# Window attention on one core: 196 padded keys replaced by a few keys that carry logarithms of exponential sums

## The reference

```python
h = layer_norm(x, ln1_g, ln1_b)
hp = jnp.pad(h, ((0, 0), (0, pad_h), (0, pad_w), (0, 0)))     # after the norm: padded keys have k = bias
qkv = win.reshape(Bw, N, C) @ qkv_w + qkv_b                    # win: 32 windows of N = 196 tokens
attn = jnp.einsum('bnd,bmd->bnm', q * scale, k)
bias_h = jnp.einsum('bhwc,hkc->bhwk', rq, Rh)                  # q times a table of row distances
bias_w = jnp.einsum('bhwc,wkc->bhwk', rq, Rw)                  # the same for column distances
attn = attn + bias_h[..., :, None] + bias_w[..., None, :]
o = jax.nn.softmax(attn, axis=-1) @ v
x2 = shortcut + o @ proj_w + proj_b
out = x2 + gelu(layer_norm(x2, ln2_g, ln2_b) @ mlp_w1 + mlp_b1) @ mlp_w2 + mlp_b2
```

## Time and profile before

| | us |
|---|---|
| median of three runs | 259.3 |
| profiled execution, own time | 261.9 |
| its span | 260.1 |
| PE busy | 243.9 (94%) |
| DVE busy | 170.0 (65%) |
| ACT busy | 128.9 (50%) |
| POOL busy | 114.7 (44%) |

### The profile page before, as it was taken

How to read it: one execution, slowest core, us unless ns; L and a number is a source line. 1 busy time by engine, 2 the same in 40 slices (tenths; PEclk the granted TensorE clock), 3 DMA queues, 4 the chain that set the end, 5 groups by cost and what they waited for, 6 DMA issues and landing times.

```text
span 260.1 us, 5439 instructions
## 1 busy us (share of the span) xinstructions
PE 243.9 (94%) x1996; PEld 190.5 (73%) x1996; DVE 170.0 (65%) x477; ACT 128.9 (50%) x216; POOL 114.7 (44%) x180
## 2 busy tenths in 40 slices
PE   7499999999799999999998989979999999999995
PEld 3245568897677777778666866658878889798994
DVE  3996839336988989988789997528977391400011
ACT  2157698436366565765657556630646451604100
POOL 4449775914116568866576653561310570000000
PEclk9889999999889999999999999977999999999999
DMA  6645214787127886777766633392000001000011
GB/s 173 188 112 138 51 36 114 177 203 174 40 66 175 188 185 168 185 178 181 196 168 152 165 82 90 97 272 70 0 0 3 0 0 61 3 30 32 14 49 62
DMA packets 22232, 27.80 MB, mean 107 GB/s; under 512 B 7287, under 2 KB 18409, under 8 KB 22205
## 3 DMA queue, kind: packets, MB, share of 16 engines
q1 hardware_dynamic: 18253, 21.37, 31.4%
q0 software_dynamic: 3424, 5.89, 9.8%
q10 hardware_dynamic: 528, 0.20, 0.3%
HBM read 5.84 MB, written 1.57 MB: 29 GB/s over the span
## 4 chain that ended last, share of the span: by engine, by line
PE 68%; DMA 11%; DVE 8%; ACT 6%; POOL 3%; issue 2%; SPq 1%; DVEq 0%; ACTq 0%; POOLq 0%
PE ps L1485 12%; PE ps L1469 8%; PE ps L1150 7%; PE ps L1259 7%; PE ps L1301 6%; PE ps L1325 5%; DMA qop<-shift 3%; DVE bias L923 3%; PE ps L1224 3%; PE ps L1382 2%; PE ps L1369 2%; DMA wq<-in_qkv_w 2%; PE ps L1330 2%; PE ps L1265 2%; DMA qop<-bias 2%
## 5 line engine op out<-in xcount | busy, mean ns | idle before, releaser
L942 DVE TENSOR_REDUCE nmax<-ps 98x2 f32<-98x392 f32 x96 | 52.6, 562 | 16.9 <-PE ps L1259 14.9
L737 ACT ACTIVATE pm<-ps 98x784 f32<-98x784 f32 x48 | 38.9, 826 | 23.6 <-PE ps L1301 23.5
L1259 PE MATMUL ps<-kop,qop 126*98 126x196 f32 x192 | 37.1, 278 | 2.1 <-DVE nmax L942 1.4
L1259 PEld LDWEIGHTS ps<-kop,qop 126*98 126x98 f32 x192 | 25.8, 168 | 9.2 <-issue 3.8
L1485 PE MATMUL ps<-w2t,gl 128*128 128x192 f32 x192 | 31.7, 326 | 0.0
L1485 PEld LDWEIGHTS ps<-w2t,gl 128*128 128x128 f32 x192 | 31.4, 190 | 0.3
L808 ACT ACTIVATE gl<-ps,vec 128x512 f32<-128x512 f32 x24 | 16.1, 686 | 30.1 <-PE ps L1469 30.1
L1301 PE MATMUL ps<-qop,kop 128*98 128x196 f32 x192 | 27.4, 266 | 0.9 <-DMA qop<-shift 0.9
L1106 DVE TENSOR_TENSOR xn<-ps,xres 128x384 f32<-128x384 f32 x8 | 4.5, 557 | 31.1 <-PE ps L1485 31.1
L1150 PE MATMUL ps<-ht,bias 128*128 128x512 f32 x48 | 22.8, 625 | 1.4 <-POOL bias L491 1.4
L1301 PEld LDWEIGHTS ps<-qop,kop 128*98 128x98 f32 x192 | 21.9, 170 | 2.7 <-DMA qop<-shift 1.3
(11 more groups left out here) (162 smaller groups left out, 500.9 us busy)
## 6 DMA issues: line engine op xcount, KB each, us to landing
qop<-bias POOLq DMA_DIRECT2D x7, 343.0 KB, 5.3
qop<-hl SPq DMA_DIRECT2D x12, 196.0 KB
kop<-hl SPq DMA_DIRECT2D x12, 196.0 KB
bias<-in_x SPq DMA_DIRECT2D x4, 384.0 KB, 4.5
xres<-in_x SPq DMA_DIRECT2D x4, 384.0 KB, 5.2
out<-xn SPq DMA_DIRECT2D x8, 192.0 KB, 1.9
kop<-kst SPq DMA_DIRECT2D x3, 477.8 KB
ot<-osb POOLq DMA_DIRECT2D x44, 32.0 KB, 2.2
```

The lines of the kernel that those rows point to most:

```text
L737: a.activation(pm[0:HALF, gi], ps[0:HALF, b0:b0 + 2, 0:2 * WIN], ACT.Exp).then_inc(s["exp_done"], 1)
L942: v_.tensor_reduce(nmax[0:HALF, h % 2, 2 * n:2 * n + 2], ps[0:HALF, bank, 0:2 * WIN].rearrange("p (t k) -> p t k", t=2), AX.X, ALU.max, ne ...
L1259: o = mm(ps[0:HALF, bank, WIN * t:WIN * (t + 1)], q[0:R_MAX, WIN * n + HALF * t:WIN * n + HALF * (t + 1)], kk[0:R_MAX, WIN * n:WIN * (n + ...
```

## The change

The padded keys' 196 scores depend on a key only through its row and its column, and each real rest token sits in a window with padded keys in a rectangle or two. A sum of exponentials over a rectangle is the product of a sum over rows and one over columns. The change computes the logarithms of these sums per query, for rows 2 to 13 and rows 0 to 1 (columns alike), and puts them on 8 more rows of q's rest part (`R_LSE`). Two keys an image (4 a pair, of which a query sees three) pick the right pair of logarithms by ones in their rows. A pair has 124 keys (`KPAIR`) in place of 120 and 196. The padded product in the rest pieces, the padded weight group, its exponential, its sums and `v_pad` go; `GROUPS` is 5.

The logarithms come in two chains, `k = 0` for eight heads in the start and `k = 1` for four heads in head 0: PE turns the position terms so that tokens are on partitions (`pad_scores_by_token`), DVE subtracts maxima (`pad_shift`), ACT takes exponentials, DVE sums (`pad_sum`), ACT takes logarithms, DVE adds the maxima back (`pad_total`), PE turns the rows back (`pad_rows_by_head`), and they are copied or split (`pad_rows_high`, `pad_rows_low`, `last_pad_rows`). POOL loads the rest rows of head 0 as well. SP loads the constants in 16 small transfers instead of 3. `LEAD` is 6, pieces are spread over the five groups by `PIECES`, the main shift rows are stored behind the third exponential instead of the fourth, and of the projections one moves behind the last sums.

```diff
-PADS = T
-KCOLS = T + WIN
+PADS_KEPT = 2
+KPAIR = PAIR + 2 * PADS_KEPT
+KCOLS = MAIN + NP * KPAIR
...
+R_LSE = R_BIAS + 4 * WS
+R_MASK = R_LSE + 8
...
-LEAD = 5
+LEAD = 6
+GROUPS = 5
+PIECES = (0, 2, 5, 8, 10, 12)
...
+                if h >= A8 and part == 1:
+                    src = hl[tq][rq:P:A8, :, MAIN:KCOLS].rearrange("p l (i t) -> p l i t", i=B)[:, :, :, 0:REST]
+                    qr = q[:, MAIN:T].rearrange("p (i t) -> p i t", i=B)
+                    for l in range(2):
+                        sp.dma_start(qr[R_HIGH + l:R_MAX:2], src[:, l]).then_inc(sl, 16)
+                    sp.dma_start(qr[0:R_BIAS], src[:, 0]).then_inc(sl, 16)
...
+            def load_biases(h, part):
 
                 n = HEADS - A8
+                c0, c1 = ((0, MAIN), (MAIN, T))[part]
+                rows_, r1 = ((WS, R_LSE), (WS + 2, R_MASK))[part]
+                if h == 1 and part == 0:
                     pool.wait_ge(s["bhi_ready"], 8)
                     pool.wait_ge(s["blo_ready"], 8)
+                if h == 0:
+                    pool.wait_ge(s["pad_high"], 2)
+                    pool.wait_ge(s["pad_ready"], 2)
                 if h == A8:
                     pool.wait_ge(s["b4_ready"], 2 * NCH)
+                if h >= RING:
+                    pool.wait_ge(s["st_done"], GROUPS * (h - RING) + (4, 5)[part])
+                if h < A8:
+                    pool.dma_start(qop[h % RING].bitcast(F32)[R_BIAS:r1, c0:c1],
+                                   bias8r.bitcast(F32)[bias_row(h):A8 * rows_:A8, :, :, c0:c1]
+                                   ).then_inc((pool_in, pool_rest_in)[part][h % RING], 16)
+                for a_ in range(2 if h >= A8 else 0):
+                    r0 = 64 * a_ + h - A8
+                    for l in range(1 - part, 2):
+                        pool.dma_start(qop[h % RING].bitcast(F32)[R_BIAS + 2 * a_ + l:r1:4, c0:c1],
+                                       bias4[r0:r0 + n * (rows_ - 1) + 1:n, l, c0:c1]
                                        ).then_inc((pool_in, pool_rest_in)[part][h % RING], 16)
...
+            load_biases(1, 0)
+            load_biases(2, 0)
+            for h in range(RING):
+                load_biases(h, 1)
...
+            def pad_exponentials(k):
+                n = (A8, HEADS - A8)[k]
+                act.wait_ge(s["pad_shifted"], k + 1)
+                x_ = pad_x[k][0:PAIR]
+                a.activation(x_, x_, ACT.Exp).then_inc(s["pad_exp"], 1)
+            def pad_logarithms(k):
+                n = (A8, HEADS - A8)[k]
+                act.wait_ge(s["pad_summed"], k + 1)
+                x_ = pad_s[k][0:PAIR]
+                a.activation(x_, x_, ACT.Ln).then_inc(s["pad_log"], 1)
+            def pad_rows_high():
+                act.wait_ge(s["pad_t_done"], 1)
+                for kind in range(2):
+                    a.copy(bias8r[3 * P // 4:P, kind, 0, MAIN:T], ps[3 * P // 4:P, 4 + kind, 0:NP * PAIR]
+                           ).then_inc(s["pad_high"], 1)
             for u in range(10):
+                if u == 4:
+                    pad_exponentials(0)
+                if u == 6:
+                    pad_logarithms(0)
+                if u == 8:
+                    pad_rows_high()
...
+                    if h == 0 and gi == 1:
+                        pad_exponentials(1)
+                    if h == 0 and gi == 2:
+                        pad_logarithms(1)
                     if gi == 0 and h:
                         output(h - 1)
-                    if gi == 3 and h + 1 < HEADS:
+                    if gi == 2 and h + 1 < HEADS:
                         store_main_shifts(h + 1)
-                    if gi == 5 and h + 1 < HEADS:
+                    if gi == 4 and h + 1 < HEADS:
                         store_rest_shifts(h + 1)
...
+            def pad_shift(k):
+                dve.wait_ge(s["pad_x_done"], k + 1)
+                if k == 0:
+                    dve.wait_ge(s["lo_ready"], 12)
+                x_, n = pad_scores(k)
+                out, m, l0 = pad_part(pad_x[k], n, WS), pad_part(pad_m[k], n, 2), 32 - 2 * n
+                v_.tensor_reduce(m[:, :, 0], x_[:, :, 2:WS].rearrange("p g r j -> p g j r"), AX.X, ALU.max)
+                after(v_.tensor_reduce(m[:, :, 1], x_[:, :, 0:2].rearrange("p g r j -> p g j r"), AX.X, ALU.max))
+                v_.tensor_tensor(out[:, :, 2:WS], x_[:, :, 2:WS],
+                                 m[:, :, 0].unsqueeze(2).to_broadcast([PAIR, 2 * NP, WS - 2, n]), ALU.subtract)
+                v_.tensor_tensor(out[:, :, 0:2], x_[:, :, 0:2],
+                                 m[:, :, 1].unsqueeze(2).to_broadcast([PAIR, 2 * NP, 2, n]), ALU.subtract
+                                 ).then_inc(s["pad_shifted"], 1)
+                v_.tensor_copy(pad_l[k][0:PAIR, :, 0:l0].rearrange("p g (r j) -> p g r j", j=n), x_[:, :, WS - l0 // n:WS])
+            def pad_sum(k):
+                n = (A8, HEADS - A8)[k]
+                dve.wait_ge(s["pad_exp"], k + 1)
+                x_, total = pad_part(pad_x[k], n, WS), pad_part(pad_s[k], n, 2)
+                v_.tensor_reduce(total[:, :, 0], x_[:, :, 2:WS].rearrange("p g r j -> p g j r"), AX.X, ALU.add)
+                v_.tensor_tensor(total[:, :, 1], x_[:, :, 0], x_[:, :, 1], ALU.add).then_inc(s["pad_summed"], 1)
+            def pad_total(k):
+                n = (A8, HEADS - A8)[k]
+                dve.wait_ge(s["pad_log"], k + 1)
+                v_.tensor_tensor(pad_l[k][0:PAIR, :, 32 - 2 * n:32].rearrange("p g (r j) -> p g r j", j=n),
+                                 pad_part(pad_s[k], n, 2), pad_part(pad_m[k], n, 2), ALU.add).then_inc(s["pad_rows"], 1)
+            def pad_rows_low():
+                for kind in range(2):
+                    dve.wait_ge(s["pad_high"], kind + 1)
+                    v_.tensor_tensor(bias8r[3 * P // 4:P, kind, 1, MAIN:T],
+                                     ps[3 * P // 4:P, 4 + kind, 0:NP * PAIR], bias8r[3 * P // 4:P, kind, 0, MAIN:T],
+                                     ALU.subtract).then_inc(s["pad_ready"], 1)
+            def last_pad_rows():
+                dve.wait_ge(s["pad_t_done"], 2)
+                for r0 in (P // 4, 3 * P // 4):
+                    v_.tensor_copy(bias4[r0:r0 + P // 4, 1, MAIN:T], ps[r0:r0 + P // 4, 6, 0:NP * PAIR]
+                                   ).then_inc(s["pad_ready"], 1)
+            pad_shift(0)
             for h in range(HEADS):
                 for n in range(B):
                     maxima(h, n)
+                    if h == 0 and n == 0:
+                        pad_sum(0)
+                    if h == 0 and n == 2:
+                        pad_total(0)
+                    if h == 0 and n == 4:
+                        pad_rows_low()
+                    if h == 2 and n == 0:
+                        pad_total(1)
+                    if h == 2 and n == 2:
+                        last_pad_rows()
...
+                    if h == 1 and n == B:
+                        pad_shift(1)
+                    if h == 1 and n == 10:
+                        pad_sum(1)
...
+            def pad_scores_by_token(k):
+                if k == 0:
+                    pe.wait_ge(s["bhi_ready"], 8)
+                    pe.wait_ge(s["blo_ready"], 8)
+                    for kind in range(2):
+                        for p_ in range(NP):
+                            for l in range(2):
+                                o = mm(ps[0:PAIR, 4 + kind, P * p_:P * p_ + A8 * WS],
+                                       bias8r[0:A8 * WS, kind, l, MAIN + PAIR * p_:MAIN + PAIR * (p_ + 1)],
+                                       ident_r[0:A8 * WS, 0:A8 * WS], start=(l == 0), stop=(l == 1))
+                else:
+                    pe.wait_ge(s["brow_ready"], 4)
+                    pe.wait_ge(s["bcol_ready"], 4)
+                    for p_ in range(NP):
+                        o = nc.tensor.transpose(ps[0:PAIR, 6, P * p_:P * (p_ + 1)],
+                                                bias4[:, 1, MAIN + PAIR * p_:MAIN + PAIR * (p_ + 1)], ident[:])
+                o.then_inc(s["pad_x_done"], 1)
+            def pad_rows_by_head(k):
+                pe.wait_ge(s["pad_rows"], k + 1)
+                for g_ in range(2 * NP):
+                    r0, bank, p_ = ((3 * P // 4, 4 + g_ // NP, g_ % NP), (32 + 64 * (g_ % 2), 6, g_ // 2))[k]
+                    o = mm(ps[r0:r0 + 32, bank, PAIR * p_:PAIR * (p_ + 1)], pad_l[k][0:PAIR, g_, :],
+                           ident[0:PAIR, 0:PAIR], start=True, stop=True)
+                o.then_inc(s["pad_t_done"], 1)
             for u in range(EARLY_V):
                 values(u)
+                if u == 3:
+                    pad_scores_by_token(0)
...
-                    c0 = MAIN + PAIR * (n - B)
-                    mm(ps[0:PAIR, bank, 0:PAIR], q[0:R_MAX, c0:c0 + PAIR], kk[0:R_MAX, c0:c0 + PAIR], start=True, stop=True)
-                    o = mm(ps[0:PAIR, bank, PAIR:PAIR + WIN], q[0:R_MAX, c0:c0 + PAIR], kk[0:R_MAX, PADS:KCOLS],
```

(43 more changed lines are left out.)

206 lines of the change are left out of this document (112 added, 94 removed).

## The result

The changed kernel took 273.6 us (median of four runs, 268.87 to 275.49) against 259.5 for the kernel before beside it: ratio 1.043, 95% interval 1.029 to 1.057. Timed again in six later runs it took 273.63, ratio 1.052 (1.047 to 1.057). The forecast was 261.4, with a range of 252.5 to 266. Medians here are of all executions of a run; ratios and intervals leave out slow executions, which lie over 1.5% above the fastest of the same kernel.

The account below looks back on a forecast made before the run. PE was taken as the bound (68% of the chain), with DVE nearly full. Losses of 8.1 us at the start against gains of 6.0 behind it gave +2.1: 264.0 us profiled, 261.4 for the median, range 252.5 to 266.

Parts of the forecast that it names:

- What goes in every head: Work leaving each head: PE would need 6.5 us of its 8.05, DVE 6.4 of its 7.22.
- the free pitch: Length of a head when no load is late: 6.8 us, PE and DVE waiting for each other through three PSUM banks.
- The ring, heads 4 to 7: Operand loads for these heads: POOL's late bias load makes s1 to s6 37.2 us instead of 40.3, gain 3.1.
- the recursion spans two heads: Wait for POOL's bias load falls mid-head, so 15.2 us pass per two heads, 7.6 a head.
- The ring, heads 8 to 11: Operand loads for these heads: SP's bias loads set 8.1 us a head, bounds 6.9 and 9.2; four heads 32.3.
- rival C: Slower on both: late loads make a pitch of 9.2 us, the start costs 1 more: 266.8 us; chance 0.14.
- The start: Logarithm chain for three keys before the first rest piece: s0, head 0's first weight group, moves 3.9 us later.
- Head 0: Carries the second logarithm chain, for four heads: 13.3 us instead of 9.13, +4.2, range 9.2 to 14.5.
- The earlier shift rows: Earlier issue of the main shift rows removes waits of 0.55 us and less; worth nothing beside the ring's pace.
- The end: Behind s11, the last head's start, the chain of output DMA, reciprocal and spread rows stays as long as before.

Follow-up runs that it names:

- e9: Changed kernel without SP's key-row loads from head 3 on, and DVE's maxima of the full pieces over half of the keys: 257.1 us, ratio 0.986.
- e3: Changed kernel without SP's two loads of key rows from head 3 on: 262.35 us, ratio 1.008.
- e4: Changed kernel without POOL's big bias loads (343 KB each) of heads 3 to 7: 266.06 us.
- e5: Changed kernel, pieces dealt (2, 2, 2, 3, 3): first piece of head h+2 behind the fourth weight group, main maxima's transpose one group later: 268.13 us.
- e7: Changed kernel, pieces dealt (2, 2, 4, 2, 2): only the main maxima's transpose moved, one group later: 274.26 us, ratio 1.055.
- the second profile: The changed kernel run and profiled once more, nothing altered: 273.63 us.
- e10: Changed kernel with both chains of the logs left out, their rows filled by four small loads: 269.81 us, ratio 1.028.
- e2: Changed kernel with a lead of five, main shift rows stored behind the fourth exponential again: 274.5 us, 5.8 us slower than without that later store.
- e17: Changed kernel, POOL's bias loads of heads 3 to 7 waiting for the next head's first weight group, two groups later: 273.85 us, ratio 1.048.
- e15: Kernel before, with POOL's bias load ahead of the split of the last biases: 266.81 us, ratio 1.015.
- e8: Changed kernel, pieces dealt (2, 2, 2, 3, 3), without SP's key-row loads from head 3 on: 265.93 us, ratio 1.023.

## Why the prediction was wrong, step by step

- **What goes in every head.** PE 6.5 us: nearly right (6.7 by e9). DVE 6.4: right (6.25). The step "I take 6.8 us as the free pitch" failed: it is 7.75 (e3, e4), and 0.62 of it is a wait of PE for DVE's parts that the new order brought (the rest, PE and DVE waiting for each other through three banks, is argued in 9). It alone made little of the error, as the ring was to hold the heads at 7.6 to 8.1 anyway: without key loads s1 to s11 is 77.1, by my sum 76.1.
- **The ring, heads 4 to 7.** This is the step that failed by most: 45.97 us for 37.2, outside the bounds that I gave (34.0 to 40.3). I let POOL's bias load alone decide and wrote that "the recursion spans two heads". Its issue is tied to the output of the head behind; SP's key loads are tied to the fourth weight group only, and with the piece moved ahead of that group their ring spans one head. Before, that ring had a head and more of room and named no wait, so I left it unpriced. It holds 1.8 to 3.0 us from the first to the last issue and 4.5 to 7.1 of landing. The place of the first pieces is worth 6.1 us (e5 against e7). The stalls are passed on: heads 1 to 5 took 7.2 us more than without key loads (45.97 for 38.8), of which the waits for key rows are 5.0 and the lower clock of two heads 2.0. The wait that I did forecast, for POOL's bias load, did not come: that load landed just as the piece was due (99.35 for 99.36 in head 2), and at 7.75 a head without key loads it was never waited for.
- **The ring, heads 8 to 11.** The right loads and the right kind of wait (bias loads of SP's queue), a size too small: 3.7 us of landing for the 3.0 that I took, and up to 4.6 from the first load to the last where I had 3.9, as SP's issues lengthened. Five stretches 42.8 for 38.9. The bounds that I gave for this ring, 6.9 and 9.2, do not follow from their own terms: 0.56 + 0.6 + 3.2 + 2.2 is 6.6, and with 4.2 and 4.1 it is 9.5, by which rival C comes to 268.0; the result lies above that too.
- **The stalls and the clock.** Not in the sum. Of the five heads that waited over 0.8 us for a load (2, 3, 4, 7 and 9) three, 3, 4 and 7, show a granted clock of 0.83 or 0.84, and PE is busy 1.0 us longer in each.
- **The start.** s0 + 3.9 forecast, + 2.7 on the second profile: mechanism right (without the chains s0 is 69.69), a bit dear; the step from 60.5 to 62.7 adds 1.14 and 0.6 and should be 62.2. The rest maximum took 281 ns (283 forecast), the maximum over 768 elements 0.96 (0.95); the sum over 768 took 1.56 for 0.95, and the start was still not dearer than forecast.
- **Head 0.** 13.3 forecast, 13.10 and 12.38 measured: the size is right, in part by luck. The sum started from 9.13, a head at clock 0.81; without the chains head 0 takes 7.79 at 1.00 (e10), so that the chains cost 4.6 to 5.3 where I took 4.2 net. PE waits 2.0 us for DVE in it (0.55, 1.07, 0.42), as forecast, and the clock, which I had left to the upper end, fell to 0.74 and 0.86.
- **The earlier shift rows.** "Worth nothing beside that" is wrong where the ring has room: 5.8 us (e2), of which the waits for shift rows are 2.2. I did not undo it in the changed kernel itself.
- **The end.** Taken as unchanged, 2.2 us shorter: 0.5 in head 11 and 1.7 behind it, where the granted clock was 0.98 against 0.96 before. Which part the moved projection has in it is not shown.
- **Rivals.** C (slower on both) had the right sign and put the loss into the late loads and the start; the key loads of heads 4 to 7 were in none of them.

## What to carry to other kernels

When work leaves a loop that refills a ring of buffers, write the ring down for every queue that refills it, not for the one that is latest now: which instruction frees the slot, which one first wants it, and whether the second stands ahead of or behind the next freeing one. If it stands ahead, the ring has the length of one turn, and here nearly all of each late microsecond was lost. Price a landing by what leaves ahead of it: here key loads that landed 3.3 us behind their issue with no big load about took up to 7.1 behind one. And read whose landing a view prints: here it was a smaller load's of the same line.

## What the runs showed of the hardware

- The last of four loads on SP's queue, 98 KB from SBUF to SBUF, landed in 3.2 to 3.7 us with no big load about (e4), in 4.5 to 7.1 with one of 343 KB issued on POOL's queue 0.3 to 2.8 us ahead of it (changed), and in 3.3 to 4.2 with the big one 1.6 to 5.1 us behind it (e17). In the kernel before it took 3.7 to 4.4 with the big load up to 0.5 us behind, and 5.2 to 5.9 with it 1.5 to 1.8 ahead (e15).
- SP's time to issue such a load, mostly 0.59 us, rose to 1.76 and 1.78 in the same stretches (L429 at 113.15 and 123.38 of the changed kernel), which made 3.0 us of the 1.84 from the first to the last main load.
- A tiny DVE operation beside POOL's cast took 0.61 to 0.62 us instead of 0.16: in three heads of e8 and three of e5 it overlapped the cast, and in none of the others. 0.7 us of PE hung on it in the three heads of e8. DVE and POOL of that kernel:
```profile
109.02 0.61 DVE L1048 TENSOR_TENSOR parts_rest<-nmax,parts_rest 120x4 fp32r<-120x4 f32 x1
```
```profile
108.94 0.67 POOL L625 CAST bias_all<-bias_all 128x512 fp32r<-128x512 f32 x1
```
